# Turning the softmax probabilities of an attention layer without TensorE: 32x32 blocks on VectorE, a block permutation by DMA, scaling on GpSimd

## The reference

```python
# z1ss, u1ss: [8, 256, 512]; 16 heads of 64; Wqkv, Winj, Wo are weights
w_heads = Wqkv @ z1ss + Winj @ u1ss              # per half of the columns, other weights
q, k, v = split(w_heads, 3, axis=1)              # each [8, 16, 64, 512]
rq = q + r_w_bias[None, :, :, None]
score = einsum('bndi,bndj->bnij', rq, k) / 8
prob = softmax(score, axis=-1)                   # [8, 16, 512, 512]
attn_vec = einsum('bnij,bndj->bndi', prob, v)
x = Wo @ attn_vec + bo + z1ss                    # then a normalisation over axis 1
```

## Time and profile before

| | |
|---|---|
| median of 3 runs | 3530.7 us |
| the profiled execution (its span) | 3531.3 us |
| PE busy | 3298.1 us, 93% |
| DVE busy | 2377.8 us, 67% |
| ACT busy | 1780.9 us, 50% |
| POOL busy | 202.5 us, 6% |
| first exponential of unit 0 / of unit 63 | 30.90 us / 1372.08 us |
| last store of the first layer issued | 1395.29 us |

### The profile page before, as it was taken

One profiled execution on the slowest core, in us unless ns is written; L12 is line 12 of the kernel. 1 busy time (PEld: TensorE's weight loads), 2 busy tenths in 40 slices (PEclk: granted clock), 3 DMA queues, 4 the chain that ended last, 5 costly groups with the idle time before them and its releaser, 6 DMA issues. The chain is left out here.

```text
span 3531.3 us, 55048 instructions
## 1 busy us (share of the span) xinstructions
PE 3298.1 (93%) x21408; PEld 2528.1 (72%) x21408; DVE 2377.8 (67%) x3781; ACT 1780.9 (50%) x4249; POOL 202.5 (6%) x319
## 2 busy tenths in 40 slices
PE   8999999999999997789999998769999999699998
PEld 6777888787777785556666655457887788488885
DVE  6666666666665665599999999537777878542213
ACT  5554444444454443446565554327777777532222
POOL 0000000000000000000000000001111111000000
PEclk9999999999999999989999999779999999899999
DMA  6322212221122211544454544130011110210004
GB/s 216 127 106 101 108 72 81 96 111 72 72 96 90 79 72 59 162 111 115 110 117 110 120 112 111 38 108 13 25 43 62 46 43 31 93 48 24 24 12 162
DMA packets 95697, 300.42 MB, mean 85 GB/s; under 512 B 20144, under 2 KB 28336, under 8 KB 70992
## 3 DMA queue, kind: packets, MB, share of 16 engines
q1 hardware_dynamic: 64960, 186.60, 18.2%
q0 software_dynamic: 12544, 79.70, 6.4%
q10 hardware_dynamic: 17936, 30.59, 2.4%
HBM read 233.95 MB, written 62.91 MB: 84 GB/s over the span
## 5 line engine op out<-in xcount | busy, mean ns | idle before, releaser
L537 ACT ACTIVATE l_prob<-l_bank,l_nmax 128x512 f32<-128x512 f32 x512 | 344.8, 686 | 276.9 <-DVE l_nmax L679 276.9
L679 DVE TENSOR_REDUCE l_nmax<-l_bank 128x1 f32<-128x512 f32 x512 | 317.3, 681 | 71.4 <-PE l_bank L409 71.3
L375 PE MATMUL l_bank<-l_x_hi,l_w_hi 128*128 128x256 f32 x1024 | 297.6, 291 | 11.3 <-DVE l_x_lo L779 11.3
L702 DVE COPY l_probT<-l_bank 128x512 f32<-128x512 f32 x256 | 173.6, 689 | 175.3 <-PE l_bank L423 174.6
L375 PE MATMUL l_bank<-l_x_hi,l_w_lo 128*128 128x256 f32 x1024 | 290.4, 284 | 0.0
L375 PE MATMUL l_bank<-l_x_lo,l_w_hi 128*128 128x256 f32 x1024 | 290.3, 284 | 0.0
L1744 DVE TENSOR_TENSOR_SCAN l_kv<-l_wx,l_kv 128x2056 f32<-128x2056 f32 x64 | 283.8, 4434 | 3.1 <-DVE l_sxc L1865 1.5
L2318 ACT ACTIVATE l2a_sc<-l2a_sc,l2a_nmax 128x256 f32<-128x256 f32 x512 | 254.8, 508 | 41.1 <-DVE l2a_nmax L2434 41.1
L423 PE MATMUL l_bank<-l_ident,l_prob 128*128 128x128 f32 x2048 | 247.9, 275 | 10.6 <-DVE l_k_lo L695 6.3
L423 PEld LDWEIGHTS l_bank<-l_ident,l_prob 128*128 128x128 f32 x2048 | 225.8, 141 | 24.3 <-DVE l_k_lo L695 16.2
L445 PE MATMUL l_bank<-l_probT,l_v 128*64 128x512 f32 x1024 | 233.8, 598 | 0.0
(11 more groups left out here) (351 smaller groups left out, 8177.3 us busy)
## 6 DMA issues: line engine op xcount, KB each, us to landing
l_vb<-vd SPq DMA_DIRECT2D x64, 1024.0 KB
l_w_hi<-kept_w_hi POOLq DMA_DIRECT2D x24, 1024.0 KB, 8.3
l_w_lo<-kept_w_lo POOLq DMA_DIRECT2D x24, 1024.0 KB, 10.3
l_wv_hi<-kept_wv_hi POOLq DMA_DIRECT2D x12, 1024.0 KB, 5.1
l_wv_lo<-kept_wv_lo POOLq DMA_DIRECT2D x12, 1024.0 KB, 7.1
kept_w_hi<-l_w_hi SPq DMA_DIRECT2D x8, 1024.0 KB, 8.7
kept_w_lo<-l_w_lo SPq DMA_DIRECT2D x8, 1024.0 KB, 11.2
l2a_x<-x SPq DMA_DIRECT2D x16, 512.0 KB, 3.6
```

Of the source, the lines that this page charges most:

```text
L375: mm = pe.matmul(s.ap[:, c * ROWS:(c + 1) * ROWS], a[:, kt, c, g, :], b[:, kt, c * ROWS:(c + 1) * ROWS], start=m == 0, stop=m == 3 * KT - 1)
L537: act.activation(prob[h][:, it, :], s.ap[:, :], ACT.Exp, bias=nmax[:, n % 2, it, h:h + 1], accum_out=rsum[:, n % 2, it, h:h + 1]).then_inc ...
L679: dve.tensor_reduce(nmax[:, n % 2, it, h:h + 1], s.ap[:, :], AX.X, ALU.max, negate=True).then_inc(max_ready, 1)
L702: dve.tensor_copy(probT[0][:, j, :], s.ap[:, :]).then_inc(s.drained, 1)
```

## The change

The turn of the probabilities leaves TensorE. It is now done in three steps.

1. GpSimd multiplies each tile by its inverse row sums in place: 8 `tensor_scalar` per unit, one for each tile and head.
2. VectorE transposes 32x32 blocks in place: one instruction per tile, both heads, 128x1024 elements. Reciprocals are now taken tile by tile.
3. A transpose within blocks leaves each block on the wrong 32 partitions. SyncE issues 32 DMAs per unit, of 32 partitions x 2 KB = 64 KB each, from `prob` to `probT`: 16 for the half made of tiles 0 and 2 (f = 0), 16 for tiles 1 and 3 (f = 1).

`prob` now has one buffer for each half, so the exponentials of a half of unit n+1 wait until all 16 DMAs of that half of unit n have landed (`half_moved`). The tiles come in the order 0, 2, 1, 3. The outputs are already normalised: two multiplications on VectorE, the copies out of banks on both engines, `turn_sums` and GpSimd's spreading go; ScalarE takes over the first parts of q and of the output. The output projection of unit n now comes in unit n+2. The product with v still comes in unit n+1, but near its end instead of near its beginning. SyncE's other transfers are placed between the moves. `wraw` shares the memory of `first_an` and `first_x`.

```diff
+    SQ, Q = 32, 4
+    TILES = (0, 2, 1, 3)
...
-        prob = [ph.sb(f"prob{h}", [P, IT, COLS]) for h in H2]
-        probT = [ph.sb(f"probT{h}", [P, IT, COLS]) for h in H2]
+        prob = ph.sb("prob", [P, 2, NB, 2, 2, SQ])
+        probT = [ph.sb(f"probT{i}", [P, 2 * Q, IT, 2, 2, SQ]) for i in range(2)]
...
+        def half_moved(eng, n, f):
+            eng.wait_ge(moved[f][n % 2], 16 * MOVES * (n // 2 + 1))
...
+                def move(n, f):
+                    sp.wait_ge(turned, IT * n + 2 * f + 2)
...
+                    if n > 1:
+                        full(sp, S[f"o{n - 2}"])
+                    for g in range(Q):
+                        for r in range(Q):
+                            sp.dma_start(probT[n % 2][r * SQ:(r + 1) * SQ, f * Q + g, :, :, :, :],
+                                         prob[g * SQ:(g + 1) * SQ, f, r * IT:(r + 1) * IT, :, :, :]).then_inc(moved[f][n % 2], 16)
...
+                for n in range(HALF):
+                    bp, pair, l = where(n)
+                    move(n, 0)
+                    move(n, 1)
+                    if bp == 0 and l == 0 and pair + 1 < HP:
+                        split_weights(pair + 1)
...
-                    pool.tensor_copy(rows[:, :, :, :], rinv[:, n % 2, :, :].unsqueeze(3).to_broadcast([P, IT, 2, D])).then_inc(rows_ready, 1)
+                    for i, it in enumerate(TILES):
+                        pool.wait_ge(rinv_ready, IT * n + i + 1)
+                        for h in H2:
+                            own = prob[:, it % 2, :, it // 2, h, :]
+                            pool.tensor_scalar(own, own, rinv[:, n % 2, it, h:h + 1], None, ALU.mult)\
+                                .then_inc(prob_ready, 1)
...
+                    for f in range(2):
+                        half_moved(pe, n, f)
+                    turned_probs = probT[n % 2][:, :, :, :, :, :].rearrange("p b t i h s -> p i b t h s")
...
-                            mm = pe.matmul(s.ap[own, :], v[l][:, pair % 2, j, own], probT[h][:, j, :], start=j == 0, stop=j == IT - 1)
+                            mm = pe.matmul(s.ap[own, :], v[l][:, pair % 2, j, own], turned_probs[:, :, :, j, h, :],
+                                           start=j == 0, stop=j == IT - 1)
...
                 def exponentials(n, its):
+                    if n:
+                        half_moved(act, n - 1, its[0] % 2)
...
+                def turns(n, it):
+                    dve.wait_ge(prob_ready, 2 * (IT * n + TILES.index(it) + 1))
+                    own = prob[:, it % 2, :, it // 2, :, :]
+                    dve.transpose(own, own).then_inc(turned, 1)
```

More of the change, by code:

```diff
@@ L172, in l0_attention @@
     order = []
-    for n in range(-1, HALF + 1):
-        if n > 0:
+    for n in range(-1, HALF + 2):
+        if n + 1 < HALF:
+            order += [f"q{n + 1}"]
+        if n > 1:
+            order += [f"w{n - 2}_0", f"w{n - 2}_1"]
+        order += {BIAS: ["cb"], CENTRE: ["nc_0", "nc_1"], VAR: ["nv"], SPREAD: ["nr"]}.get(n, [])
+        if n + 1 < HALF:
+            order += [f"k{n + 1}"]
+        if 0 < n <= HALF:
             order += [f"o{n - 1}"]
         if n + 1 < HALF:
[L177 to L184, removed]
+            order += [f"v{n + 1}_0", f"v{n + 1}_1"] if where(n + 1)[1] % 2 == 0 else []
     plan = [(label, 4 + i % 4) for i, label in enumerate(order)]
-    plan += [(f"s{n}_{it}{h}", 2 * (it % 2) + h) for n in range(HALF) for it in range(IT) for h in H2]
+    plan += [(f"s{n}_{it}{h}", 2 * (i % 2) + h) for n in range(HALF) for i, it in enumerate(TILES) for h in H2]
     def scratch(name, shape):
@@ L646, in _ @@
                     bp, pair, l = where(n)
-                    exponentials(n, (0, 1))
-                    exponentials(n, (2, 3))
+                    if n > 1:
+                        outputs(n - 2)
+                    exponentials(n, TILES[0:2])
+                    if n + 1 < HALF:
+                        queries(n + 1)
+                    exponentials(n, TILES[2:4])
                     if n == 0:
@@ L669, in _ @@
                         normed()
+                for n in (HALF - 2, HALF - 1):
+                    outputs(n)
                 act.wait_ge(xn_ready, RT)
@@ L684, in queries @@
                     full(dve, s)
-                    dve.tensor_scalar(q_hi[l][:, :], s.ap[:, :], rb[:, pair:pair + 1], None, ALU.add).then_inc(q_hi_ready, 1)
                     dve.wait_ge(q_hi_ready, n + 1)
@@ L789, in _ @@
                     bp, pair, l = where(n)
-                    maxima(n, (0, 1))
-                    if n:
-                        outputs(n - 1)
-                    maxima(n, (2, 3))
+                    maxima(n, (TILES[0],))
+                    if n > 1:
+                        outputs(n - 2)
+                    maxima(n, (TILES[1],))
+                    reciprocals(n, (TILES[0],))
+                    turns(n, TILES[0])
+                    reciprocals(n, (TILES[1],))
                     if n + 1 < HALF:
                         queries(n + 1)
-                    if n:
-                        add_up(n - 1)
+                    maxima(n, (TILES[2],))
+                    turns(n, TILES[1])
+                    maxima(n, (TILES[3],))
+                    reciprocals(n, (TILES[2],))
+                    if n > 1:
+                        add_up(n - 2)
+                    if n + 1 < HALF:
+                        keys(n + 1)
                     if bp == 0 and l == 0 and pair + 1 < HP:
@@ L960, in l1_layer @@
         ident = ph.sb("ident", [P, P])
-        eps, power, an, x, cb = [first[name] for name in ("eps", "power", "an", "x", "cb")]
+        eps, power, cb = [first[name] for name in ("eps", "power", "cb")]
+        an, x = first["anx"][:, 0, :, :], first["anx"][:, 1, :, :]
         own_rows, other_rows, ncol = [first[name] for name in ("own_rows", "other_rows", "ncol")]
```

166 lines of the change are left out of this document (70 added, 96 removed).

## The result

The changed kernel takes 3870.4 us (median of 4 runs, 3867.0 to 3878.5) against 3531.9 us for the kernel before beside it: a ratio of 1.0965, 95% interval 1.0947 to 1.0983. It is 338 us slower; 73 us faster was forecast, and the time lies above the range too.

What follows compares the result with a forecast made beforehand. TensorE bounds the kernel before; the loop through the DMAs, 18.3 us, replaces it. 30.9 + 63 x 18.7 + 40 + 30 + 10 + 33.5 = 1322.5 against 1395.3: 73 us less, 3458 us, range 3325 to 3605.

Steps and rivals of the forecast that it cites:

- What bounds the kernel before, and what leaves TensorE: TensorE's work sets the unit, mean 20.9 us; 36 transposes, 4.02 us a unit, leave it, mean then 16.9.
- both rings: VectorE's own loop, forecast to close at 17.4 us, and SyncE's issue of 32 transfers, forecast at 15.4 us a unit.
- The new loop: Path from one exponential of a half to the next through VectorE, GpSimd and SyncE's DMAs: 18.3 us, replacing TensorE's 16.9.
- GpSimd's multiplication: One multiplication of 128x512 on GpSimd, taken at 0.82 us, bounds 0.61 and 1.39.
- Rival 2: GpSimd's multiplications at 1.39 us each decide: 21.5 us a unit, 108 us slower, 3639 us; chance 0.23.
- Its turning point: Multiplication time on GpSimd, about 1.15 us, or 19.85 us a unit, from which GpSimd decides and the kernel is slower.
- SyncE's pace: Time SyncE needs to issue each 64 KB DMA, taken at 0.48 us: 7.2 us from first to last of 16.
- the one rival on it: SyncE issues at 0.39 us, TensorE stays the bound: about 17.3 us a unit, 187 us less, 3344 us; chance 0.20.
- GpSimd's work on tile 2 runs beneath these: In half 0, GpSimd's multiplications of tile 2, 5.75 to 7.4 us, hidden under VectorE's reciprocals, `l_q_lo` and maxima.
- the prediction's own sum: Half 0's steps from its first exponential to the last DMA's landing, with four handovers: 18.3 us.
- What is added besides: Beyond the loop: splits 40 us, large transfers 30, TensorE's clock 10, and a tail of 33.5 against 23.2 before.
- The rule on issue: Issue time on the sequencer is usually small beside the DMA; by it the loop would be 13.6 us and TensorE the bound.

Runs made afterwards that it cites:

- e3: Changed kernel with GpSimd multiplying only 2 of 512 columns and 4 transfers a half in place of 16: 3450.6 us.
- e6: Changed kernel with GpSimd multiplying only 2 columns, 4 transfers a half and no reload of the split weights: 3343.6 us.
- e13: Changed kernel with GpSimd's multiplication written as tensor_tensor with the reciprocal broadcast, nothing left out: 3778.2 us.
- e1: Changed kernel with GpSimd multiplying only 2 of the 512 columns of each tile and head: 3734.5 us.
- e2: Changed kernel with each half carried by 4 transfers of 128 partitions in place of 16 of 32: 3724.3 us.
- e5: Changed kernel without the reload of the split weights for the second to fourth pair of batch elements: 3778.8 us.
- e8: Changed kernel with the multiplication on ScalarE and half 1's 16 transfers issued by GpSimd, half 0's by SyncE: 3651.6 us.
- e10: Changed kernel with the multiplication on ScalarE and each half's 16 transfers shared, 8 on SyncE and 8 on GpSimd: 3576.3 us.

## Why the prediction was wrong

**What bounds the kernel before, and what leaves TensorE**: right. With both rings short (e3, e6) TensorE did not need its 20.9 us; units of 14.8 us appear, and e6 has 18.2 on average. The product with v costs what it did at full clock: its 16 matmuls take 3.65 us in each of the 28 units in which they ran at clock 1.00, and the mean of 749 ns comes from the others.

**The steps that failed are two sizes in "The new loop", and an overlap that rested on the first.** The first is GpSimd's multiplication. I had one row of the operation itself, 552 ns for 128 columns, and drew the slope from the copy, 0.69 ns a column; it is 2.5. The upper bound used the slope of a two-input operation, 2.18, as if one input could not be slower; it is. Rival 2 had the mechanism right, and got 0.23 for an argument by likeness. Its turning point, 1.15 us, no run confirms: at 1.04 us (e13) the kernel is still 7% slower than before, as the issue is too slow as well. The second is SyncE's pace, 0.48 us from transfers with one side in DRAM, for transfers with both sides in SBUF: 0.67. No bound was put on it from above at all; the one rival on it went below. The overlap is "GpSimd's work on tile 2 runs beneath these": with 3.1 us for two multiplications it does not, and the second transpose waits 1.16 us for it.

Put into the prediction's own sum, they give 18.3 + 1.5 (two multiplications 3.13 instead of 1.64) + 1.2 (the wait of the second transpose) + 2.3 (15 steps of issue at 0.63 instead of 0.48) + 0.1 (transposes): 23.4 us. The shortest units take 22.2, since GpSimd starts 1.8 us after the first exponential and not 2.7. That is near the 22.3 us that VectorE's ring takes and near SyncE's 21.5. The structure of the loop was right. Since all three lie together, neither size alone explains the loss, as e1, e2 and e13 show.

**What is added besides.** The layer ended at 1733.5 (its last store; 1322.5 was forecast), 411 us later: 2.5 at the start, 9.9 in the tail (43.4 us from the last unit's first exponential for 33.5), 398.5 in 63 units. Of these, 63 x (22.3 - 18.7) = 227 are the two sizes. The reload takes 92 where 30 stood, 62 more, though 75 was given as the bound of all large transfers. Some 110 us remain. The residual's wait is 14 of them; how the rest divides between splits, the inputs' loads and the clock (0.87 instead of 1.00) no run separates, and it stays open. The trace of e5, without the reload, shows only where it lies: the first 16 units, in which the weights are split, take 26.8 us on average, 72 us over 22.3 in all, where 40 were forecast for the splits; the other 47 take 24.2, 87 us over in all, spread over many units. Why a small transfer lands late behind a large one stays open too: it is not the packets' size, and one reload spread over more units is no cheaper.

**The rule on issue** ("DMA: Bandwidth & Descriptors", section "Issuing engines are not separate DMA queues", of the Trainium skill: initiating on several engines saves only sequencer time, usually small beside the transfer) does not hold in its second part for this kernel: the sequencer's time is not small, and e8 saved 165 us and e10 75 more by a second issuing engine. The prediction was right to leave it.

**Range.** Its top, 3605, lay inside rival 2 (3538 to over 3640). A multiplication beyond the bound, a slower issue and dearer large transfers all point the same way, and were counted as if only one could come.

## What to carry to other kernels

Price an operation on GpSimd and the issue of a transfer from a row of the same operation with the same kinds of operands, and where there is none, take the dearest neighbour as the centre, not as the bound. When work leaves a saturated engine for a chain through three others and a queue, write down the length of each ring it closes: rings of nearly one length hide each other in experiments, and only undoing both shows them. A unit that waits for many small transfers also starts to pay for large ones that were free.

## What the runs showed of the hardware

- SyncE issued a transfer every 0.46 us from DRAM to SBUF, 0.56 from SBUF to DRAM (0.47 to 0.49 for the 1 MB stores of the kernel before) and 0.63 from SBUF to SBUF (up to 0.67 on average in the layer); the last holds for 16 KB as for 256 KB. GpSimd needed 0.49 to 0.50 for this last kind.
- A transfer of 64 KB from SBUF to SBUF landed 2.0 us after its issue, and 5.4 to 9.9 us after it behind 2 or 4 MB of loads issued just before.
- GpSimd's `tensor_scalar` in fp32 (1.56 us for 128x512) is slower than its `tensor_tensor` with a broadcast operand (1.04) and its copy (0.61), and at 1024 columns (2.84) slower than its `tensor_tensor` of two full inputs (2.49). The Trainium skill ("GPSIMD Engine Reference", section "3.1 Elementwise — side-by-side cycle accounting") has a two-input `tensor_tensor` dearer per element than its best loop, which takes 769 ns for 512 elements; here `tensor_scalar`, with one tensor as input, is the dearer one, and the copy takes less than 769 ns.
- VectorE's block transpose in fp32 took 1.245 us for 1024 columns, about the rate of its other operations (0.69 for 512, 2.29 for 2048).
